# Graph-layer passes: a single float32 context product per graph in place of split products for left and right

## What is computed

```
u = einsum('bid,bjd->bij', h, h) / sqrt(D)
delta = softmax(u) * adjacency
attn = delta / (sum(delta) + 1e-10)
hl, hs, hr = h @ wl.T + bl, h @ ws.T + bs, h @ wr.T + br
ctx = (attn * upper) @ hl + diag(attn) * hs + (attn * lower) @ hr
h = relu((ctx - mean(ctx)) / sqrt(var(ctx) + 1e-12) * g + beta)
```

## Time and profile before

| what | value |
| --- | --- |
| median of 3 runs (lowest to highest) | 2837.92 us (2832.22 to 2837.97) |
| the profiled execution, its own time | 2831.32 us |
| span of the profiled execution, mean granted PE clock | 2829.6 us, 0.976 |
| busy over the span: PE, PEld | 2625.7 us (93%), 2333.2 us (82%) |
| busy over the span: DVE, ACT, POOL | 2167.9 us (77%), 1445.6 us (51%), 1920.3 us (68%) |
| graph pass l20, from its first weight transposes to those of l21 | 1204.45 to 1676.30 us |
| graph pass l21, to the first weight transposes of l3 | 1676.30 to 2198.11 us |

### The profile page before, as it was taken

The page is one execution under the profiler, slowest core; times in us unless marked ns, Lnnn a source line. Parts: engine busy times, 40 slices in busy tenths (PEclk is TensorE's granted clock), DMA queues, the critical chain, the costliest instruction groups (busy, mean ns, idle before and its releaser), DMA issues. The chain is left out here.

```text
span 2829.6 us, 67112 instructions
## 1 busy us (share of the span) xinstructions
PE 2625.7 (93%) x22942; PEld 2333.2 (82%) x22942; DVE 2167.9 (77%) x3795; ACT 1445.6 (51%) x2968; POOL 1920.3 (68%) x2229
## 2 busy tenths in 40 slices
PE   7999999977999999689999979999898899999997
PEld 6888888866777777589999978888887688888886
DVE  4888888874888888757777757888888478888887
ACT  4555555535555555344444434445544455555553
POOL 2777777772666656657777748888887277777776
PEclk9999999998999999889999989999999999999999
DMA  3222222112222222131212122222321122222211
GB/s 106 72 69 68 70 68 68 60 48 86 83 74 76 74 73 75 56 99 57 68 55 66 56 97 75 82 78 77 91 77 56 56 69 72 68 70 68 68 60 49
DMA packets 179135, 200.54 MB, mean 71 GB/s; under 512 B 56517, under 2 KB 179017, under 8 KB 179017
## 3 DMA queue, kind: packets, MB, share of 16 engines
q1 hardware_dynamic: 179016, 198.99, 22.8%
HBM read 136.03 MB, written 62.91 MB: 70 GB/s over the span
## 5 line engine op out<-in xcount | busy, mean ns | idle before, releaser
L418 PE MATMUL l_ps_p<-l_xT,l_w 128*128 128x512 f32 x2592 | 678.7, 407 | 16.7 <-ACT l_qT L559 8.7
L1097 PE MATMUL l_ps_h<-l_w,l_hT 128*128 128x384 f32 x3456 | 676.1, 341 | 0.0
L1097 PEld LDWEIGHTS l_ps_h<-l_w,l_hT 128*128 128x128 f32 x3456 | 606.0, 189 | 2.0
L418 PEld LDWEIGHTS l_ps_p<-l_xT,l_w 128*128 128x128 f32 x2592 | 468.8, 189 | 124.0 <-ACT l_qT L559 16.0
L345 POOL TENSOR_TENSOR l_pr<-l_sc,l_st 128x768 f32<-128x768 f32 x192 | 283.0, 1474 | 390.4 <-DVE l_st L693 390.4
L315 POOL TENSOR_TENSOR v<-v,l_bvs 128x768 f32<-128x768 f32 x192 | 375.6, 1957 | 0.0
L1005 POOL TENSOR_TENSOR l_hp<-l_hf,l_hp 128x384 fp32r<-128x384 f32 x256 | 282.3, 1103 | 132.2 <-ACT l_hp L1189 128.6
L412 PE MATMUL l_ps_p<-l_w,l_xT 128*128 128x384 f32 x1728 | 341.5, 344 | 21.1 <-ACT l_k L565 17.6
L578 ACT ACTIVATE v<-l_ps_p 64x192 f32<-64x192 f32 x768 | 249.0, 324 | 175.5 <-PE l_ps_p L412 168.4
L700 DVE TENSOR_REDUCE l_st<-l_pr 128x12 f32<-128x768 f32 x192 | 182.8, 952 | 202.8 <-ACT l_pr L611 200.0
L1189 ACT ACTIVATE l_hp<-l_hf 128x384 fp32r<-128x384 f32 x256 | 134.5, 525 | 397.8 <-DVE l_hf L1314 397.5
(11 more groups left out here) (129 smaller groups left out, 4701.2 us busy)
## 6 DMA issues: line engine op xcount, KB each, us to landing
rows<-l_yo SPq DMA_DIRECT2D x256, 192.0 KB, 1.9
l_xa<-rows SPq DMA_DIRECT2D x64, 768.0 KB, 5.1
l_xr<-rows SPq DMA_DIRECT2D x192, 192.0 KB, 2.4
l_xa<-in_x SPq DMA_DIRECT2D x16, 768.0 KB, 5.1
l_xr<-in_x SPq DMA_DIRECT2D x64, 192.0 KB, 2.4
out<-l_yo SPq DMA_DIRECT2D x64, 192.0 KB, 1.9
l_edge<-in_adj SPq DMA_DIRECT2D x80, 128.0 KB, 2.3
raw<-in_L_gnn_Wq SPq DMA_DIRECT2D x3, 576.0 KB, 5.8
```

The costliest lines, as they stand in the source:

```text
L418: last = nc.tensor.matmul(bank[:, :], W[m][:, l, t, o * P:(o + 1) * P], rows[:, r, t, :], start=c + t == 0, stop=c == 2 and t == KT - 1)
L1097: last = nc.tensor.matmul(ps_h[m][:, :D], hT[gpar][:, l, t, s * P:(s + 1) * P], W[m][:, r, t, :], start=c + t == 0, stop=m != SELF and c = ...
```

## The change

Only `digcn_pass` and what it calls is touched. Projections and attention weights are no longer rounded or split for the context.

- DVE forms attn (128x64 per unit) and, with one product against a 0/1 tile halves, a tile wide of 128 columns per unit: for a row i of graph g, the block of 64 columns with number g holds its entries j > i (for the left projection), the other block its entries j < i. `attention_T` transposes it; one ACT copy (L1179 of the new file) takes ps_a to aT. The masked products, their rounding and their low parts are gone.
- ACT copies ps_h0 and ps_h1 straight into a stacked tile hlr (L1189): for graph g one 64-row half holds the left rows, the other half the right rows. Each is two copies of 64x384.
- POOL adds both biases to the whole stack, 128x768, in place (`side_biases`, L1005, L1009), once for both sides.
- The context is one float32 matmul per graph, 128x64 weights by 384 columns, each into its half of ps_c (L1111), and it stands behind RIGHT instead of before it.
- On POOL the add stands before the inner bundle.

The core of the diff (removed and new waits of the same kind are left out):

```diff
-                pe.wait_ge(pool_h, 2 * (n + 1))
+                pe.wait_ge(pool_h, n + 1)
...
-                for m in range(2):
-                    for c, (l, r) in enumerate(SPLIT):
-                        last = nc.tensor.matmul(ps_c[:, :D], aT[gpar][:, m, l, s, :], hp[s % 2][:, m, r, :],
-                                                start=m + c == 0, stop=m == 1 and c == 2)
+                for g in range(GPU):
+                    q = slice(g * NODES, (g + 1) * NODES)
+                    last = nc.tensor.matmul(ps_c[q, :D], aT[gpar][:, s, q], hlr[s % 2][:, g, :], start=True, stop=True)
...
                     project(n, i, par, s, LEFT)
                     if s == 0:
                         rows_T(i + 1, 1 - par, (0,))
+                    project(n, i, par, s, RIGHT)
                     context(n - 1, ppar, ps)
-                    project(n, i, par, s, RIGHT)
...
             def left_right(n, b, m):
-                act.wait_ge(dve_h, 2 * n + m + 1)
+
+                act.wait_ge(pe_h, 3 * n + m + 1)
                 if counted(n - 1):
                     act.wait_ge(pe_c, n - 1)
-                nc.scalar.activation(hp[b][:, m, 0, :], hf[b][:, m, :], ACT.Copy).then_inc(act_h, 1)
+                for g in range(GPU):
+                    half = (g + m) % 2
+                    i = nc.scalar.activation(hlr[b][half * NODES:(half + 1) * NODES, g, :],
+                                             ps_h[m][g * NODES:(g + 1) * NODES, :D], ACT.Copy)
+                i.then_inc(act_h, 1)
...
+            def side_biases(n, b):
+
+                pool.wait_ge(act_h, 3 * n + 2)
+                pool.wait_ge(s_small, 16 * n_small)
+                nc.gpsimd.tensor_tensor(hlr[b][:, :, :], hlr[b][:, :, :], sides[:, :, :], ALU.add).then_inc(pool_h, 1)
...
-                    left_right(n, s % 2, LEFT)
                     if s == 0:
                         rows_low(i + 1, 1 - par, (0,))
+                    side_biases(n, s % 2)
                     rstd(n - 1, (s - 1) % 2, epsi, 6, dve_mv, pool_ve, pool_rs)
-                    left_right(n, s % 2, RIGHT)
...
+                    nc.vector.tensor_tensor(attn[:, :, :], u4[:, :, :], st[:, 5, :].unsqueeze(2).to_broadcast([P, UNITS, NODES]),
+                                            ALU.mult).then_inc(dve_attn, 1)
...
-                    for b in range(GPU):
-                        q = slice(b * NODES, (b + 1) * NODES)
-                        nc.vector.tensor_tensor(wide[q, :, b * NODES:(b + 1) * NODES], u4[q, :, :],
-                                                st[q, 5, :].unsqueeze(2).to_broadcast([NODES, UNITS, NODES]),
-                                                ALU.mult).then_inc(dve_wide, 1)
+
+                    nc.vector.tensor_tensor(wide[:, :, :, :], attn[:, :, :].unsqueeze(2).to_broadcast([P, UNITS, 2, NODES]),
+                                            halves[:, :, :].unsqueeze(1).to_broadcast([P, UNITS, 2, NODES]),
+                                            ALU.mult).then_inc(dve_wide, 1)
...
-                    for m, mask in enumerate((after, before)):
-                        nc.vector.tensor_tensor(part[m][:, :, :], ps_a[:, :].rearrange("p (u q) -> p u q", u=UNITS),
-                                                mask[:, :].unsqueeze(1).to_broadcast([P, UNITS, P]), ALU.mult).then_inc(dve_part, 1)
...
-                nc.vector.tensor_tensor(hf[b][:, m, :], ps_h[m][:, :D], sides[:, m, :], ALU.add).then_inc(dve_h, 1)
```

More of the change, by code:

```diff
@@ L826, in digcn_pass @@
         bias = a.sb("bias", [P, D], F32R)
-        sides = a.sb("sides", [P, 2, D])
+        sides = a.sb("sides", [P, GPU, D])
         gain = a.sb("gain", [P, D])
@@ L833, in digcn_pass @@
         same = a.sb("same", [P, NODES])
+        halves = a.sb("halves", [P, 2, NODES])
         xa = a.sb("xa", [P, UNITS, D])
@@ L844, in digcn_pass @@
         diag = [a.sb(f"diag{b}", [P, UNITS]) for b in range(2)]
-        wide = a.sb("wide", [P, UNITS, P])
-        part = [a.sb(f"part{m}", [P, UNITS, P]) for m in range(2)]
-        aT = [a.sb(f"aT{b}", [P, 2, 2, UNITS, P], F32R) for b in range(2)]
-        hf = [a.sb(f"hf{b}", [P, 2, D]) for b in range(2)]
-        hp = [a.sb(f"hp{b}", [P, 2, 2, D], F32R) for b in range(2)]
+        attn = a.sb("attn", [P, UNITS, NODES])
+        wide = a.sb("wide", [P, UNITS, 2, NODES])
+        aT = [a.sb(f"aT{b}", [P, UNITS, P]) for b in range(2)]
+        hlr = [a.sb(f"hlr{b}", [P, GPU, D]) for b in range(2)]
         hs = [a.sb(f"hs{b}", [P, D]) for b in range(2)]
@@ L899, in _ @@
                 sp.dma_start(brow[row:row + 1, :], row_biases[SELF]).then_inc(s_small, 16)
-            for m in (LEFT, RIGHT):
-                sp.dma_start(sides[:, m, :], row_biases[m].to_broadcast([P, D])).then_inc(s_small, 16)
+            for g in range(GPU):
+                for m in (LEFT, RIGHT):
+                    half = (g + m) % 2
+                    sp.dma_start(sides[half * NODES:(half + 1) * NODES, g, :],
+                                 row_biases[m].to_broadcast([NODES, D])).then_inc(s_small, 16)
             sp.dma_start(gain[:, :], ln_scale.to_broadcast([P, D])).then_inc(s_small, 16)
@@ L951, in _ @@
             nc.gpsimd.tensor_tensor(same[:, :], ident[:, 0:NODES], ident[:, NODES:P], ALU.add).then_inc(c_mask, 1)
+            pool.wait_ge(c_mask, 3)
+            for g in range(GPU):
+                q = slice(g * NODES, (g + 1) * NODES)
+                nc.gpsimd.tensor_copy(halves[q, g, :], before[q, q]).then_inc(c_mask, 1)
+                nc.gpsimd.tensor_copy(halves[q, 1 - g, :], after[q, q]).then_inc(c_mask, 1)
+            pool.wait_ge(c_mask, masks)
             def attention(g, gpar, step):
@@ L1148, in _ @@
             over_groups(pe, groups, group)
-            ga[0] = 2 * groups
+            ga[0] = groups
             context(units - 1, 1, UNITS - 1)
@@ L1252, in _ @@
             nc.vector.memset(bias[:, :].bitcast(F32), 0.0).then_inc(c_zero, 1)
-            nc.vector.memset(wide[:, :, :], 0.0).then_inc(c_zero, 1)
             for step in range(steps):
@@ L1361, in inner_norm @@
                                                op0=ALU.mult, op1=ALU.add).then_inc(dve_o, 1)
-            for step in range(5):
+            for step in range(4):
                 attention(0, 0, step)
@@ L1368, in group @@
                     n, b = i * UNITS + s, s % 2
-                    left_right(n, b, LEFT)
                     context(n - 1, 1 - b)
@@ L1372, in group @@
                         attention(i + 1, 1 - par, 1)
-                    left_right(n, b, RIGHT)
                     if s == 3:
                         attention(i + 1, 1 - par, 3)
-                        attention(i + 1, 1 - par, 4)
                     if ends:
```

79 lines of the change are left out of this document (32 added, 47 removed).

## The result

| | before | after |
|---|---|---|
| median of the runs, us | 2835.3 (4 runs, 2832.2 to 2838.0) | 2863.3 (4 runs, 2862.4 to 2865.6) |
| profiled execution, span | 2829.6 | 2862.2 |
| first graph pass, period of a group | 27.93 | 27.16 |
| second graph pass, period of a group | 30.73 | 33.55 |

A forecast was written before the change was run, and what follows sets the result against it. PE was taken to bound the first pass, a POOL and ACT cycle the second; -2, 0 and +0.6 us at the starts sum to -1.4: 2830 from the own time 2831.3, 2836 from the median; range over the cases 2797 to 2872.

The forecast's parts named there:

- the ring: Second graph pass: a closed cycle of POOL and ACT steps sets the pace, 6.65 us per unit, 26.6 per group before extras.
- PE's wait at attention_T: First graph pass: PE stands 0.8 us (0 to 1.2) per group for DVE's wide tile.
- the add: POOL's one bias add of 128x768 per unit: 1.96 us, bounds 1.47 to 2.21.
- have less to do or the same: Second graph pass: does not move, 0 us, although all four engines have less work or the same.
- PE waiting at the context for POOL's add: Second graph pass: a sign that would show the forecast right; no size given.
- Together 4.3, so the ring takes 30.9 us per group: Second graph pass: row copies, attention copy and POOL's outer-bundle delays add 4.3 to 26.6, against 30.87 before.
- On half the partitions and of the same length: ACT's copies in the first pass's attention_T chain: two 64-row copies priced at 0.87 us, like the earlier pair.
- the attention chain: First graph pass, from RIGHT's end in unit 2 to attention_T: 7.6 us, including about 0.6 behind DVE's normalisation step.
- rival 3: Second graph pass: add at 2.21 us and bundles waiting 0.2 us for the port; period 33.1, +35 us, 2870; 22%.
- First pass: First graph pass: PE work 27.0 plus 0.8 us stand gives period 27.8, 0.13 us less per group, gaining 2 us.
- Rival 4: PE's matmuls run in strict order, so a context takes about 0.33 us more: first pass +8 us, 2846; 6%.
- Rivals 1 and 2: PE sets the pace everywhere, 77 us less, 2761 (12%); or the add costs only 1.47 us, 2800 (15%).

The follow-up runs named there:

- e2: Changed kernel plus one unread ACT copy of 384 columns behind hs in every unit of the second graph pass: 2886.9 us, second-pass period 34.96.
- e1: Changed kernel plus the same unread ACT copy, placed between RIGHT's copies and standardise in the second graph pass: 2865.8 us, second-pass period 33.50.
- e3: Changed kernel with POOL's inner bundle before the add instead of behind it in the second graph pass: 2822.5 us, second-pass period 30.77.
- e7: Changed kernel without VectorE's gain and shift steps of the inner norm in the second graph pass: 2845.8 us, second-pass period 32.12.
- e6: Changed kernel with one ACT copy of 128 rows per side instead of two of 64 in the second graph pass: 2820.9 us, second-pass period 30.58.
- e4: Changed kernel with PE's attention_T moved from before to behind SELF of unit 3 in both graph passes: 2848.7 us, periods 26.66 and 32.90.
- e9: Kernel before the change, with POOL's inner bundle moved behind RIGHT's low part in the second graph pass: 2890.3 us, second-pass period 34.38.
- e5: Changed kernel with the edits of e3 and e4 together: 2783.9 us, ratio to the kernel before 0.9798 to 0.9830, second-pass period 28.60.

## Why the prediction was wrong

**Where it was right.** The step that decides is the ring, "add(n), inner bundle(n-1), standardise(n-1), hs(n), left copies(n+1), normed(n-2), right copies(n+1), add(n+1)". It is there link by link (54 waits of 54; e2 in it, e1 beside it; e3 cuts it). That the pass gains nothing from PE's and POOL's smaller work was right too, and so were PE's wait at attention_T in every group of the first pass and the add: 1.94 us, forecast 1.96. Two things were not right. The four engines do not all "have less to do or the same": ACT's four copies a unit replace two. And the sign "PE waiting at the context for POOL's add" did not come in the second pass, where PE stood at attention_T (3.4 us a group) and at the row products (1.25) instead.

**The step that failed** is the ring's sum, "Together 4.3, so the ring takes 30.9 us per group", taken as equal to the 30.87 of before. It is 33.55. For the group shown above, whose period is 33.88, link by link against the forecast:

| link | forecast | measured, in the units where it decides | per group |
|---|---|---|---|
| standardise to hs | 0.61 | 0.61, 0.74 | +0.1 |
| left pair | 0.78 | 1.00, 0.99 | +0.4 |
| normed to right copies | 0.60 | 0.73, 0.72, 0.73, 0.74 | +0.5 |
| right pair, to the add | 0.87 + 0.07 | 1.06 four times | +0.5 |
| add | 1.96 | 1.80, 1.80, 2.01, 2.21 | 0.0 |
| bundle, to standardise | 1.25 + 0.04 | 1.27, 1.58, 1.76, 1.95 | +1.4 |
| standardise to normed, from unit 1 to 2 and 2 to 3 | 2.66, 3.01 | 2.53, 3.12 | 0.0 |

Together +2.9 us, about half on ACT and half in the bundle. (Over all groups the adds come out 0.3 us below the forecast, and the period at 33.55.) In the last row the prediction had POOL's outer bundle decide both places. It decides the second; in the first ACT's own rows take 2.53 us, with an exp of 0.32 us that the sum did not name, and normed has no wait there (14 waits for the bundle in the window of 54 units, one a group). The size came out by chance. Two things were mis-sized. **The copies and their neighbours**: the price came from the earlier trace rows, two copies of 128 rows that overlap by 0.1 us. "On half the partitions and of the same length" was right (483 ns for 64 rows and for 128), but the two of a pair follow each other at 0.485 us without overlap, and the row behind them starts only when they have ended. **The bundle**: the earlier trace rows is a bundle for which no VectorE step was in line. Behind the add, in three units of four, the bundle's first step takes 0.50 us instead of 0.19, to the end of a VectorE step that was issued while the add ran; with two of VectorE's steps a unit left out (e7) the bundles are 1.4 us a group shorter. The prediction used this very effect in the attention chain ("should stand for about 0.6") and in rival 3, and left it out of the ring's sum. e6 takes away more than was mis-sized, the whole second copy of a pair, and so gives 3.0.

**Rival 3** had the sign, the place and nearly the period (33.1). Its price was the add at 2.21 and 0.2 us a bundle; the add stayed at 1.94, the bundles paid more, and half of the loss was on ACT, which it did not name. The ring's links were taken from rows without a neighbour that disturbs, and such a sum is nearer to a lower end than to a middle. That the total still lies in the stated range is luck: the second pass, at 33.55, is outside the prediction's own bounds for it (28.9 to 33.1), and the first pass gained 12 us where 2 were forecast, which covers it.

**First pass.** Forecast -0.13 us a group, measured -0.77. The context took 0.7 to 0.8 us start to start, not 0.90: below the lower bound of 0.81, which came from a burst of 24 records where this one has 4. PE's work is 26.66 (e4), not 27.0, and the stand 0.53, not 0.8. Rival 4, strict order on PE, wanted 0.33 us more than 0.90 for a context and falls. Rivals 1 and 2 are answered by the period of 33.55.

**What the order of the change did.** Putting the inner bundle behind the work of RIGHT costs 2.8 us a group in the new kernel (e3) and 3.65 in the old one (e9), so the loss is not the price of the float32 context. It is not the order alone either: with the order kept, one copy a side instead of two takes it away as well (e6, 3.0 us a group). The split copies cost time because they stand in the ring; a copy beside it was free (e1). The new arithmetic with the bundle first and attention_T later (e5) is 1.9% faster than the kernel before; the second of these moves was not tried in the old kernel.

## What to carry to other kernels

When a change moves a step behind another in one engine's queue, write down the cycle that this closes with the other queues, and sum it with rows of the same shape and the same neighbours: a copy split in two halves counts twice, and a bundle behind a long POOL operation pays for the VectorE step that was released meanwhile. Where no engine is full, put one small instruction into the suspected ring and then beside it: the pair tells a ring from an amount of work before anything is moved.
